# Issuing the zeros for the result rows only after expert 0's gathered rows have landed, in a fused recurrent block with a mixture of experts

## The reference

```python
xn = _layernorm(x)
# branch 1: a gated recurrence over each sequence
x_conv = causal_depthwise_conv(xn)                  # 4 taps
r_t, i_t = sigmoid(x_conv @ W_r.T + b_r), sigmoid(x_conv @ W_i.T + b_i)
a_t = sigmoid(log_a) ** (8.0 * r_t)
h_t = a_t * h_(t-1) + sqrt(1 - a_t**2) * i_t * x_conv
attn = rmsnorm(h @ W_out.T) * gamma
# branch 2: top-1 mixture of 8 experts, at most 512 rows for each
eidx = argmax(softmax(xn @ Wr)); rank = position of the row among the rows of its expert
xe = xn[dispatch]                                   # (8, 512, 128), a gather by row
ye = relu(xe @ W1[e]) @ W2[e]                       # 128 -> 512 -> 128
y = zeros((4096, 128)).at[dispatch].add(ye * p)     # a scatter by row
out = x + attn + y
```

## Time and profile before

| what | value |
|---|---|
| device time, median of 3 | 130.85 us (130.85 to 131.13) |
| span of the profiled execution | 128.8 us |
| busy share PE, DVE, ACT, POOL | 82%, 79%, 77%, 66% |
| transfers | 19.27 MB, mean 150 GB/s |
| the zeros, SP's issue | from 20.54 us |
| first gather issued by POOL | 25.89 us |

### The profile page before, as it was taken

One profiled execution on the slowest core, in us unless ns is written; L12 is line 12 of the kernel. 1 busy time (PEld: TensorE's weight loads), 2 busy tenths in 40 slices (PEclk: granted clock), 3 DMA queues, 4 the chain that ended last, 5 costly groups with the idle time before them and its releaser, 6 DMA issues.

```text
span 128.8 us, 2229 instructions
## 1 busy us (share of the span) xinstructions
PE 106.2 (82%) x711; PEld 89.9 (70%) x711; DVE 101.8 (79%) x238; ACT 99.6 (77%) x219; POOL 84.6 (66%) x109
## 2 busy tenths in 40 slices
PE   3999999999799999999999997999997999700000
PEld 3999976672379779789879987898697899600000
DVE  5398998999699999979614489999999975973690
ACT  3299792888589589789689999999999799823560
POOL 8987774078788787778777877888787878700000
PEclk9999999999999999999999999999999999998555
DMA  2966964892456365312611711111110111149995
GB/s 85 383 247 173 405 244 173 318 380 66 103 169 181 80 209 139 118 53 56 209 41 41 219 51 41 61 37 41 52 57 25 60 43 61 41 108 302 325 372 215
DMA packets 8234, 19.27 MB, mean 150 GB/s; under 512 B 1689, under 2 KB 1945, under 8 KB 8224
## 3 DMA queue, kind: packets, MB, share of 16 engines
q1 hardware_dynamic: 5424, 13.70, 31.5%
q0 software_dynamic: 2080, 4.19, 11.2%
q10 hardware_dynamic: 720, 1.25, 2.6%
HBM read 10.82 MB, written 8.39 MB: 149 GB/s over the span
## 4 chain that ended last, share of the span: by engine, by line
PE 60%; DVE 9%; DMA 8%; ACT 8%; issue 5%; POOL 4%; POOLq 1%; SPq 1%; DVEq 0%; ACTq 0%
PE bank L624 17%; PE bank L609 6%; PE bank L611 6%; PE bank L610 6%; DMA dec<-y_rows 4%; PE bank L640 4%; PE bank L453 3%; PE bank L561 3%; PE bank L442 3%; POOL xn_tok L405 3%; DMA xn_tok<-xn_rows,idx_in 2%; ACT xc L796 2%; PE bank L594 2%; PE bank L563 2%; PE bank L562 2%
## 5 line engine op out<-in xcount | busy, mean ns | idle before, releaser
L405 POOL DMA_INDIRECT xn_tok<-xn_rows,idx_in x32 | 33.7, 1054 | 14.4 <-issue 9.4
L417 POOL DMA_INDIRECT y_rows<-xn_tok,idx_out x32 | 33.5, 1047 | 9.7 <-issue 9.1
L624 PE MATMUL bank<-w_raw,h_sb 128*128 128x128 f32 x256 | 29.9, 275 | 0.0
L624 PEld LDWEIGHTS bank<-w_raw,h_sb 128*128 128x128 f32 x256 | 29.2, 192 | 0.0
L786 ACT ACTIVATE h_sb<-bank 128x512 f32<-128x512 f32 x32 | 18.8, 598 | 2.5 <-PE bank L611 0.6
L609 PE MATMUL bank<-xg_hi,w_hi 128*128 128x512 f32 x32 | 13.2, 412 | 0.0
L611 PE MATMUL bank<-xg_hi,w_lo 128*128 128x512 f32 x32 | 12.6, 393 | 0.0
L610 PE MATMUL bank<-xg_lo,w_hi 128*128 128x512 f32 x32 | 12.5, 391 | 0.0
L1021 DVE SCALAR_TENSOR_TENSOR xc<-xnT,par,xc 128x1020 f32<-128x1020 f32 (+2 forms) x9 | 11.5, 1277 | 0.3
L640 PE MATMUL bank<-par,xc 128*128 128x128 f32 x64 | 8.8, 280 | 2.2 <-ACT xc L796 1.3
L1061 DVE TENSOR_TENSOR_SCAN xnT<-dec,bank 128x256 f32<-128x256 f32 x16 | 10.1, 674 | 0.3
(11 more groups left out here) (143 smaller groups left out, 243.2 us busy)
## 6 DMA issues: line engine op xcount, KB each, us to landing
w_raw<-in_weights SPq DMA_DIRECT2D x8, 512.0 KB, 3.9
y_rows<-sca SPq DMA_DIRECT2D x4, 512.0 KB, 5.9
dec<-y_rows SPq DMA_DIRECT2D x8, 256.0 KB, 5.7
x_tok<-in_x SPq DMA_DIRECT2D x3, 512.0 KB, 5.9
xn_rows<-xn_tok SPq DMA_DIRECT2D x3, 512.0 KB, 3.6
out<-dec SPq DMA_DIRECT2D x4, 256.0 KB, 3.1
out<-dec ACTq DMA_DIRECT2D x4, 256.0 KB, 2.9
x_tok<-in_x SPq DMA_DIRECT2D x2, 256.0 KB, 3.5
```

Source lines behind the costliest of these rows:

```text
L405: g.indirect_dma_start(gathered[:, s * D:(s + 1) * D], None, xn_rows, bass.IndirectOffsetOnAxis(ap=idx_in[:, s:s + 1], axis=0)).then_inc(g ...
L417: g.indirect_dma_start(y_rows, bass.IndirectOffsetOnAxis(ap=idx_out[:, s:s + 1], axis=0), gathered[:, s * D:(s + 1) * D], None, bounds_che ...
L624: last = mm(tile_of(e, s), h_sb[:, k * CAP + s * P:k * CAP + (s + 1) * P], w_raw[:, e, F + k * D:F + (k + 1) * D], start=(k == 0), stop=(k ...
```

## The change

SP waits, before it issues the first transfer of zeros, until all four slices of expert 0's gather have landed.

```diff
             sp.wait_ge(zeroed, 1)
+            sp.wait_ge(gather_in[0], 16 * ST)
             for c in range(C):
                 sp.dma_start(y_rows[c * TC:(c + 1) * TC, :].rearrange("(p j) d -> p (j d)", p=P),
                              zeros).then_inc(zero_out, 16)
```

## The result

| | us |
|---|---|
| before, median of 4 | 130.85 (129.75 to 131.13) |
| changed, median of 4 | 135.0 (133.64 to 138.13) |
| ratio | 1.0245, 95% interval 1.0175 to 1.0316 |
| span of the profiled execution, before and changed | 128.8 and 131.6 |

The forecast was 130.9 us in a range of 130.1 to 132.2. Timed again in twelve executions, the changed kernel had a median of 134.07 us against 130.81, and a single one of them, at 130.93, was no slower than before. So the loss is some 3 us in the median and differs much from one execution to the next.

What follows compares the result with a forecast made beforehand. POOL's uninterrupted issue stream was taken to set the end. Second slice (0 to -0.3, taken as 0), PE stall, ACT and POOL all 0 left the span at 128.8 us; with 2.05 around it, 130.9 us, range 130.1 to 132.2.

Steps and rivals of the forecast that it cites:

- a cover at expert 6's first half: Room between DVE's copy and POOL's scatter, less the 0.30 gap: 1.24 us of PE lateness that costs nothing.
- (a): Expert 1's gather beside the moved zeros: PE stalls 0 to 2.2 us, taken as 0.2, under the cover: 0.
- The rival of 0.13: At `turn(1)`, gather 1 is held to the end of the backlog: +1.0, 131.9 us; chance 0.13.
- All three signs of being wrong: PE's transposes of expert 1 behind 40.3, a POOL wait on a copy, or POOL's slice sum changed by over 0.4 us.
- The rule on turns between queues: Skill's packet-by-packet turns: gather 1's landing would stay put, term 0; the prediction held that two trace windows disagree.
- (b): `decay(0)` on ACT waits for all zeros; landing at 40.0 to 42.0, free until 41.66, at most 0.35 us back: cost 0.
- (c): Work queued behind the new wait, and POOL's issue of six slices beside full queues: -0.7 to +1.8 us, taken as 0.
- two of the rivals: POOL issues slower beside the zeros, 131.6 to 132.4 us, chance 0.18; POOL is freed, 129.9 to 130.6, chance 0.20.
- The long second slice: First gather's second slice on POOL, 1.27 us; if the old zeros slowed it, 0 to -0.3 us, taken as 0.

Runs made afterwards that it cites:

- the run without ACT's wait: Changed kernel with the zeros in the last quarter of the buffer, so ACT waits for them only before the square of chunk 3; 133.93 us, ratio 1.0255.
- the run with PE late: Kernel before, zeros in their old place, PE's transposes of expert 1 also waiting for DVE's taps of chunk 2; 133.93 us against 130.74.
- The run with eight transfers: Changed kernel with the same zeros in eight transfers of 256 KB in place of four of 512 KB; 137.22 us.
- eight transfers and no wait of ACT: Changed kernel with zeros in eight 256 KB transfers and ACT's wait moved from decay 0 to the square of chunk 3; 131.26 us against 130.91.
- one transfer: Changed kernel with the zeros in one transfer of 2 MB; 136.62 us against 130.81.

## Why the prediction was wrong

**What sets the end: right, with the cover mis-sized.** POOL's stream does set it, and a delay of PE counts only beyond a cover at expert 6's first half, where the prediction put the smallest. It took the cover as 1.24 us, from POOL's start less a gap of 0.30. The traces give 0.72 (the times leave some room for more, as said): a wait that POOL really has to make costs it 0.82 from the end of the copy (104.31 to 105.13), not 0.30. In the rows of before no such wait stood. And POOL's stream is not as free as the prediction had it, as the fixed distance of eleven traces shows.

**The step that failed: (a), expert 1's gather.** "For the slice at 35.19 I take +1.0 to +1.6 over 2.6, in place of its 3.3: landing at 38.8 to 39.4". It landed at 42.5, 6.7 us after its issue, or +4.1, and PE stalled 3.07 us where the sum had 0.2. The holds that I read, 1.0 and 1.6 us, were those of a slice beside the end of the zeros and beside a single weight load, both with little behind them. With four transfers and a weight load in the queue, the later slices of a gather wait longer than the first. The upper bound, a wait for the whole of zeros and weights to 41.3, was nearer, and still too low. Its mechanism was not quite the case: the last slice landed with the last zeros and not behind the weights (in the run without ACT's wait at 42.4, with the weights issued just before it at 44.4). What made it too low is the rate: it ran the zeros at 410 GB/s from 34.2 to 39.3, where they landed by about 42.6 (35.1 + 7.5), in windows of 281 to 383 GB/s:

```profile
34.00:36.00 2.00, 2.00 (x8) 0.96 (x7) 1.22 (x3) 1.41 (x3) 1.39 (x3) 1.00 0.79 281
36.00:38.00 2.00, 2.00 (x11) 1.63 (x10) 2.00 (x6) 1.82 (x4) 1.70 (x2) 1.00 0.99 383
```

**The rival of 0.13 was the case.** Its place was right; its price of +1.0 should have been 3.44 - 0.72 = 2.7. It took the lateness of PE 1.2 us too small (2.2 for 3.44) and the cover 0.5 too wide, and both made it look harmless. All three signs of being wrong that the prediction named came: PE's transposes behind 40.3, waits of POOL on a copy, and POOL's slices 1.1 us longer in sum (-0.6 and +1.7).

**The rule on turns between queues.** The Trainium skill, in DMA: Bandwidth & Descriptors, section Queues, rings and completion order, has each DMA engine take turns packet by packet, and puts a packet at about 9 to 17 descriptors. The prediction took one packet of the profile, 4 KB, for one turn. Turns as small as that are not what the trace of the changed kernel shows: a slice, 64 KB, took 6.7 us beside SP's queue. That the rule itself is wrong is not shown. A transfer of 512 KB has 128 rows of 4 KB, eight for each of 16 engines; as an estimate from the page's figure that is close to one packet, and turns by such packets would look like the turns by whole transfers that fit the landings above. No run here tells what counts as a packet.

**ACT's wait (b): right for this kernel.** `decay(0)` starts at 43.70 right behind the split of gather 1, not behind the zeros, and the run without its wait is as slow. But its cover ended at 41.66 and its upper bound was 42.0, and the zeros landed at 42.6; it was hidden only by the larger stall. The run with eight transfers shows it as the next wait.

**POOL beside full queues (c): right.** The gathers' mean fell from 1054 to 1033 ns. Most of the 0.6 us is one slice: that of 39.08, 1.69 us long, on which two of the rivals rested in part, takes 1.01 or 1.02 in every other trace, also where the weights are issued as before. So it was no work of the weights beside it. The scatters' 1.7 us more are for 0.94 the first scatter behind a wait, 2.02 us, as in the run with PE late; the rest lies in single long slices elsewhere. The long second slice is no work of the zeros: 1.27 in the changed kernel with none in flight.

**What was not counted:** that a PE left idle may come back at half its clock. It costs 1.6 us in the traces where it does, and by that widens the spread of the changed kernel.

## What to carry to other kernels

Before a block of transfers is moved, look which small, late-issued transfer runs beside its new place and how much room its consumer has; here 2 MB cost nothing beside gathers 2 and 3, and 3 us beside gather 1. A hold read beside a short queue is a lower bound for a long one: cost it by all that was issued before the held transfer, at the rate that mixed traffic reaches. An edit that cuts the same bytes into other transfers also changes when they are issued; look at that before the size is given the credit. Where one engine issues without a pause, room measured to its next start less its usual gap overstates the cover, as a wait that is really made costs more than the gap.

## What the runs showed of the hardware

- A gather on POOL's queue is held for several us beside transfers of SP's queue: a slice of 64 KB that takes 2.6 us on free engines took 5.3 to 6.7 in the changed kernel, its landings one for one with those of SP's transfers of 512 KB. With the same bytes cut otherwise PE started at 39.99 or 41.91 us (256 KB, two executions), 42.52 (512 KB) and 43.83 (2 MB).
- SP took 8.50 us to issue eight transfers of 256 KB and 2.12 us to issue four of 512 KB at the same place.
- A first scatter that POOL had to wait for took 2.02 us in each of the eight traces in which it waited (0.88 to 3.77 us), and 1.08 in those in which it did not. Behind the later wait, at expert 6, the scatter took 0.97 as always. Why only the first is long is open.
- The clock behind a stall of PE differs between executions of one kernel: in the changed kernel 1.00 after 3.07 us and 0.50 after 3.00. In other runs it was 1.00 after 3.27 (PE late) and 0.50 after 1.90 (eight transfers and no wait of ACT) and 4.20 (one transfer). The low clock cost 1.6 us in each of these three traces at 0.50.
